# Sixteen-head attention: from two score banks and two banks of turns to three and one, on one core of a Trainium2

## What is computed

```python
# first layer (stage l0a): 16 heads of width 16, masked by a bias on the keys
x = x + _L0_xattn_ref(ctx_2048, _layernorm(x), L0_xattn_b, itok)
# sixth layer (stage l2s): causal self-attention, 16 heads of width 16
scores = jnp.einsum('bhqd,bhkd->bhqk', q, k) * HD ** (-0.5)
scores = jnp.where(causal[None, None], scores, -jnp.inf)
attn = jax.nn.softmax(scores, axis=-1)
ao = jnp.einsum('bhqk,bhkd->bhqd', attn, v)
```

## Time and profile before

| | |
|---|---|
| median of three runs | 3182.69 us (3179.83 to 3188.03) |
| the profiled execution's own time | 3181.22 us |
| its span | 3179.5 us |
| PE busy | 2534.5 us (80%) |
| DVE busy | 2180.8 us (69%) |
| ACT busy | 1264.9 us (40%) |
| POOL busy | 996.3 us (31%) |
| stage l0a, first score to last division | 64.1 to 307.8 us |
| stage l2s, first score to the next stage's first turn | 1941.7 to 2167.1 us |

### The profile page before, as it was taken

The page is one execution under the profiler, slowest core; times in us unless marked ns, Lnnn a source line. Parts: engine busy times, 40 slices in busy tenths (PEclk is TensorE's granted clock), DMA queues, the critical chain, the costliest instruction groups (busy, mean ns, idle before and its releaser), DMA issues. The chain is left out here.

```text
span 3179.5 us, 57281 instructions
## 1 busy us (share of the span) xinstructions
PE 2534.5 (80%) x21348; PEld 1651.8 (52%) x21348; DVE 2180.8 (69%) x5526; ACT 1264.9 (40%) x2260; POOL 996.3 (31%) x1420
## 2 busy tenths in 40 slices
PE   2997285999904497997989876886799999969972
PEld 1443263666603266886556543444466555656662
DVE  6897763666547764766678767997666545867758
ACT  1786353333212313111346654773322222256621
POOL 3442271110066170112656316874000000024330
PEclk9999597999956599998999987998899999989996
DMA  4331266221171026665721022100100000011001
GB/s 104 122 120 58 91 237 203 80 73 63 45 249 31 24 97 233 234 224 185 243 78 48 18 72 82 43 23 6 64 9 12 1 1 1 1 42 52 22 9 58
DMA packets 158167, 266.90 MB, mean 84 GB/s; under 512 B 22635, under 2 KB 106137, under 8 KB 151876
## 3 DMA queue, kind: packets, MB, share of 16 engines
q1 hardware_dynamic: 131204, 186.97, 17.8%
q0 software_dynamic: 17904, 76.23, 7.1%
q10 hardware_dynamic: 8784, 0.04, 0.2%
HBM read 175.25 MB, written 88.34 MB: 83 GB/s over the span
## 5 line engine op out<-in xcount | busy, mean ns | idle before, releaser
L1427 ACT ACTIVATE l2e_hf<-l2e_H 128x512 f32<-128x512 f32 x208 | 124.2, 597 | 376.1 <-PE l2e_H L1383 376.1
L1552 POOL TENSOR_TENSOR all_m_rstd<-all_m_sq,all_mhalf 128x8 f32<-128x8 f32 x18 | 29.6, 1646 | 551.0 <-DVE all_m_sq L1537 550.9
L731 DVE TENSOR_REDUCE l0a_mx<-l0a_S 128x2 f16<-128x512 f32 x256 | 168.3, 688 | 24.0 <-PE l0a_S L565 23.3
L1463 DVE CAST l2e_hh<-l2e_hf 128x512 f16<-128x512 f32 x208 | 88.8, 427 | 125.8 <-ACT l2e_hf L1427 110.7
L727 DVE CUSTOM_DVE_ANT_0 l2s_masked<-l2s_S,l2s_mq 128x128 f32<-128x128 f32 (+1 forms) x512 | 153.2, 349 | 19.9 <-PE l2s_S L565 19.5
L680 ACT ACTIVATE l0a_pf<-l0a_ST 128x512 f32<-128x512 f32 x256 | 146.7, 602 | 45.3 <-PE l0a_ST L579 45.0
L1383 PE MATMUL l2e_H<-l2o_hi,l2e_w 128*128 128x512 f16 x576 | 151.8, 382 | 14.9 <-DVE l2e_w L1439 14.9
L1427 ACT ACTIVATE l0e_hf<-l0e_H 128x512 f32<-128x512 f32 x128 | 76.4, 597 | 207.2 <-PE l0e_H L1383 207.2
L1383 PE MATMUL l2e_H<-l2e_hh,l2e_w 128*128 128x512 f16 x640 | 155.1, 379 | 0.0
L1383 PE MATMUL l1e_H<-l1b_hi,l1e_w 128*128 128x256 f16 (+1 forms) x936 | 144.7, 274 | 7.8 <-DMA l1e_w<-packed,all_second_weight_row 7.8
L1465 DVE TENSOR_TENSOR l2e_hl<-l2e_hf,l2e_hh 128x512 f16<-128x512 f32 x208 | 144.0, 693 | 7.2
(11 more groups left out here) (713 smaller groups left out, 7541.3 us busy)
## 6 DMA issues: line engine op xcount, KB each, us to landing
l0e_wf<-in_L_ffn_w SPq DMA_DIRECT2D x16, 1024.0 KB, 7.2
rows<-l0a_zeros SPq DMA_DIRECT2D x16, 640.0 KB, 5.9
l1u_rb<-rows SPq DMA_DIRECT2D x20, 512.0 KB, 5.2
results<-l1e_y SPq DMA_DIRECT2D x39, 256.0 KB, 3.8
l0a_kv<-in_ctx SPq DMA_DIRECT2D x16, 512.0 KB, 4.1
rows<-l0a_zeros SPq DMA_DIRECT2D x16, 512.0 KB, 4.9
l0d_p_cx<-in_ctx SPq DMA_DIRECT2D x16, 512.0 KB, 6.7
l0u_rb<-rows SPq DMA_DIRECT2D x16, 512.0 KB, 5.7
```

Of the source, the lines that this page charges most:

```text
L731: m = nc.vector.tensor_reduce(mx[h % 2][:, :, i], ps[:, :].rearrange("p (u k) -> p u k", u=TB), AX.X, ALU.max)
L1427: nc.scalar.activation(hf[q % 4][0:fn, :], pair_of(q, lay)[0][0:fn, :], lay.func, scale=1.0 / WS).then_inc(acted, 1)
L1463: nc.vector.tensor_copy(high, v).then_inc(hi_done, 1)
L1552: self.nc.gpsimd.tensor_tensor(out=(self.rstd, self.rstd2)[which][:, g], in0=(self.sq, self.sq2)[which][:, g], in1=self.g.mhalf[:, 0:self. ...
```

## The change

With 16 heads the stage gets a third score bank and gives up the second bank of turns: queries, keys and maxima are all turned in one bank, in that order round, each turn waiting for the copy of the one before. LAG grows from 17 to 19, both halves of `weigh` stand in the same slot (0 and 4, where c = 0 stood in 2 and 6 and c = 1 in 4 and 0), `turn_back` moves from slot 1 to 2, `copy_max` from 4 to 3, `divide` from 3 to 4, `copy_keys` from 1 to 0, and `copy_queries` from slot 0 of the next group to slot 6 of the same group. The stages with 8 heads keep every value.

```diff
-    LAG = heads + 1
+    LAG = 19 if heads == 16 else 9
+    SR = 3 if heads == 16 else 2
     RING, VR, NPF = 6, 5, 3 * G
-    BACK_AT, MAX_AT, TURN_Q_AT, TURN_K_AT = (1, 2, 5, 7) if heads == 16 else (1, 1, 3, 3)
-    COPY_AT, DIV_AT, KEYS_AT, SUM_AT = (4, 3, 1, 5) if heads == 16 else (2, 3, 1, 3)
-    APART = G // 2 if heads == 16 else 0
+    BACK_AT, MAX_AT, TURN_Q_AT, TURN_K_AT = (2, 2, 5, 7) if heads == 16 else (1, 1, 3, 3)
+    COPY_AT, DIV_AT, KEYS_AT, SUM_AT = (3, 4, 0, 5) if heads == 16 else (2, 3, 1, 3)
+    QUERIES_AT, QUERIES_FOR = (6, 2) if heads == 16 else (0, 1)
+    APART = 0
...
-        S_ps = [st.ps(f"S{i}") for i in range(2)]
+        S_ps = [st.ps(f"S{i}") for i in range(SR)]
...
-        MH_ps = [st.ps(f"M{i}", [P, 8, P], F16) for i in range(2)]
+        MH_ps = [st.ps(f"M{i}", [P, 8, P], F16) for i in range(1 if heads == 16 else 2)]
+        if heads == 16:
+            MH_ps = MH_ps * 2
...
-                        if n >= 2:
-                            pe.wait_ge(maxed, n - 1)
-                    m = pe.matmul(S_ps[n % 2][:, s_at[u]:s_at[u] + key_to[u]],
+                        if n >= SR:
+                            pe.wait_ge(maxed, n - SR + 1)
+                    m = pe.matmul(S_ps[n % SR][:, s_at[u]:s_at[u] + key_to[u]],
...
                     if h:
                         pe.wait_ge(q_turned, h)
+                        if heads == 16:
+                            pe.wait_ge(k_turned, h)
                     turn(h, 0)
...
                     if h:
                         pe.wait_ge(k_turned, h)
+                    if heads == 16:
+                        pe.wait_ge(q_turned, h + 1)
                     turn(h, 1)
...
                     pe.wait_ge(q_turned, min(h + 3, NH))
+                    if heads == 16:
+                        pe.wait_ge(k_turned, min(h + 3, NH))
...
-                    ps = S_ps[n % 2]
+                    ps = S_ps[n % SR]
...
-                    if i == 0 and 0 <= j + 1 < NH:
-                        copy_queries(j + 1)
+                    if i == QUERIES_AT and 0 <= j + QUERIES_FOR < NH:
+                        copy_queries(j + QUERIES_FOR)
```

## The result

The changed kernel takes 3188.8 us (median of 20 runs) where the kernel before takes 3183.6 us in the same comparison (20 runs): a ratio of 1.0018, with a 95% interval of 1.0011 to 1.0025. That is 5 us or 0.2% slower. By the bound of 0.3% it counts as no change, but the interval leaves out 1, so the sign is settled. The forecast was 3175 us with a range up to 3185.

A forecast was written before the change was run, and what follows sets the result against it. No engine is full; a loop of waits between TensorE and VectorE sets each group's period. Stage l0a at -11.1 us and l2s at +3.8 us make -7.3 us, so 3175 us against the median of 3182.7, range 3159 to 3185 us.

The forecast's parts named there:

- The old loop: In l0a before: copy of maxima, turn of queries, TensorE to slot 3's score, maximum, division, copy again; 7.15 us per group.
- path B: Loop around one group over ScalarE's copy of the keys and the first exponential: 6.81 us in l0a, 6.52 in l2s.
- Path A: Loop around one group over the paired `weigh` on TensorE and VectorE's maxima: 6.79 us in l0a, 6.36 in l2s.
- So a group of l0a takes 6.80 us.: Period of a group in l0a after the change, 0.35 us less than before; 26 groups give -9.1 us.
- the ring: One bank's cycle: turn of queries, VectorE's copy, turn of keys, ScalarE's copy, turn of maxima, VectorE's copy; handoffs 0.05 us.
- rival 3: Each handoff of the bank costs 0.15 us, not 0.05: +17 us, 3192 us; decides from 0.11 us on; chance 0.06.
- Every second group takes 6.9 us, the mean is 6.71.: In l2s the pair of slot 4 waits for GpSimd's later cuts: 0.16 us more per group, +4.2 us in 26.
- LAG of 19 adds two slots with exponentials alone at each end: At the ends of each stage, slots with exponentials alone cost 0.5 to 0.6 us each: +1.2 us per stage.
- The first four groups: At each stage's start the third score bank frees VectorE: -3.5 and -0.9 us in l0a, -3.3 us in l2s.
- the last two groups: At each stage's end these groups turn nothing and gain: -2.0 us in l0a, -1.5 us in l2s.
- Rival 2: Engines overlap almost fully: groups of l0a at VectorE's 6.15 us and of l2s at 5.88, 3135 us; chance 0.07.
- Rival 4: TensorE's clock falls to 1.2 GHz where it waits more often: 1.9 us more per group, +48 us in one stage; chance 0.02.

## Why the prediction was wrong

**Right.** The old loop ends, and the loop through the one bank of turns sets the period, over two paths that nearly tie (7.00 us over B, 6.93 over A). The pair holds TensorE 156.30 - 155.30 = 1.00 us, VectorE idles 0.63 us (forecast 0.7) ahead of the maximum of slot 1, the copied keys start 0.03 us behind the turn of keys, the start costs 3.2 us in each stage, and l2s loses by GpSimd's stacking in every second group. The run with later copied keys bears out that last step: with the first exponential ahead of the copied keys, l2s goes to 6.40 us in every group.

**Wrong: sizes, all with one sign.** The step that failed is the sum around the loop, above all *"So a group of l0a takes 6.80 us"*. The two stages missed by 11.3 us (+4.0 for -7.3). The other 2.5 us between 3175 and 3188.8 us lie outside them or in the scatter of executions.
- *"So a group of l0a takes 6.80 us."* It takes 7.00, which is 5.3 us in 26 groups. Of the 0.20 us, the handoff from the copy of the queries to the turn of keys makes 0.09: 0.14 us, where I took 0.05 with a bound of 0.10. Turning back and turned maxima took 0.79, the bound, and not 0.73: the overlap of 0.06 us that I called my estimate isn't there. These two lie on path B, which decides; the maxima and the first exponential add the rest, 0.01 to 0.03 us each. Path A by itself is 6.93 us for 6.79: the same handoff, and four maxima at 2.41 for 2.34. The other two handoffs of the ring are 0.03 and 0.06 us. So rival 3 (0.15 us each, all three) has one of its three, and the mean of 0.08 stays below its point of 0.11.
- *"Every second group takes 6.9 us, the mean is 6.71."* It is 6.67 and 6.99, mean 6.83; with the table's +6.2 for +4.2 that is 2.0 us. (The periods alone would give 3.1 us; single groups at both ends of the stretch differ from them, and one group of before took 7.12 us.) The short group has nearly the same handoff, 0.15 us: TensorE starts the turn of keys at 2032.46, the copy ended at 2032.31.
- *"LAG of 19 adds two slots with exponentials alone at each end, ... 1.2 us."* 2.1 and 2.3 us, 2.0 us more in all. I had not costed the pairs there. The end of l0a on ScalarE, after:

```profile
287.88 2.24 ACT L690 ACTIVATE l0a_pf<-l0a_ST 128x512 f32<-128x512 f32 x4 [0.72 <-PE l0a_ST L583]
290.47 0.60 ACT L684 ACTIVATE l0a_oT<-l0a_O 128x512 f32<-128x512 f32 x1 [0.36 <-PE l0a_O L599]
...
296.45 0.60 ACT L684 ACTIVATE l0a_oT<-l0a_O 128x512 f32<-128x512 f32 x1 [0.36 <-PE l0a_O L599]
```

and before:

```profile
295.77 0.60 ACT L674 ACTIVATE l0a_oT<-l0a_O 128x512 f32<-128x512 f32 x1
...
301.49 0.60 ACT L674 ACTIVATE l0a_oT<-l0a_O 128x512 f32<-128x512 f32 x1
```

  Behind each pair ScalarE waits 0.72 us for the next ST. A group at the end takes 296.45 - 290.47 = 5.98 us; before it took 5.72 us. By my estimate from these rows, two slots more at 0.75 us (5.98 / 8) and two groups 0.26 us longer make 2.0 of l0a's 2.1 us; no run separates them.
- *The first four groups* gained 6.2 us in both stages together and not 7.7, and the last two groups 3.0 and not 3.5. Both were worked out with the same short path A; I take that for the cause, without a run for it.

These add up to 11 us, the error of the two stages. The range was too narrow for the same reason: I bounded the handoff (too low, at 0.10 us) and GpSimd's wait and let the other estimates stand, though most were taken at their lower end, and the sum of a loop multiplies such an error by 52 groups.

Two slips in the rivals decided nothing. Rival 2's sum for VectorE in l2s is 5.91 us, not 5.88, and the chance of a gain over 0.3% comes to 0.44, not 0.43. Rival 4 took the price of the low clock from a turn of 1.01 us, but for 60 to 70 us of that trace the granted clock is given as 1.00 too, so that row doesn't show the price.

**What the prediction didn't weigh.** It named three causes for the gain in one sentence ("together they cost less") and never asked what each is worth. The runs did. Three of them and the change make a chain from before to after, in which each line is one run and changes only what it names against the line above it (the usual period of a group in l0a and, on average, in l2s; then the two stages together and the step; all in us):

```
                                          l0a    l2s    stages   step
before                                    7.15   6.55    494.5
copy of maxima first, division later      6.72   6.34    475.6  -18.9
three score banks, one bank of turns,
  copied queries in slot 6                7.01   6.48    490.3  +14.7
pairs, LAG of 19, turning back later      6.93   6.40    485.5   -4.8
copied keys in slot 0 (the change)        7.00   6.83    498.5  +13.0
```

The steps hold in this order and need not in another. With two score banks the pairs cost 0.56 us per group of l0a (7.28 for 6.72), and in the change's own slots 0.28 us (7.00, the run with two banks of turns, whose copied keys are in slot 0 too). So the change is one gain of 19 us and a small one of 5, and two losses, the exchange of banks and the copied keys ahead of the first exponential, that give them back. The prediction foresaw how the copied keys make GpSimd late in l2s, but never asked what slot 1 would give.

The Trainium skill (TensorEngine Tiling, Key Properties) says that a change of tiling mode drains TensorE. The trace still agrees: one such change less is 0.14 us per pair, seen in the 1.00 us above. It is a saving in an engine that isn't the bound. The fall of the clock that rival 4 took up, and that the Trainium skill (TensorE: Matmul & The Clock Gate, A second HAM failure mode: psum-queue depth-cycling) describes for another kernel, didn't come: the granted clock stays 1.00 in both stretches with three score banks.

## What to carry to other kernels

Where two engines are both near 90% busy and wait for each other once per group, find the one instruction that the loop waits for and move that alone first: here a copy of 0.2 us moved ahead of a division of 0.6 us, with the division a slot later, was worth 0.7%, and what was built around it lost the gain again. A bank taken from one use and given to another moved the wait here and didn't remove it; trace the ring of the use that gives before counting what the other gets. Joining two pieces of work saved the engine that does them, but while they lasted the engines fed by it got nothing, so count the banks that are to bridge it. And where a change moves several constants, put each back alone: one of them, a copy of 1.0 us ahead of an exponential that a third engine waits for, cost 13 us of the 19 gained.

## What was not expected

- A handoff isn't one number. From VectorE's copy of 1024 elements (0.68 us by its row) to TensorE's first turn it is 0.14 to 0.15 us; from TensorE's turn to ScalarE's copy 0.03, from an exponential to TensorE 0.06.
- A pair, 128x32 tiles with 16 matmuls, holds TensorE 1.00 us in l0a and 2034.05 - 2033.26 = 0.79 us in l2s (forecast 0.80); where the turned maxima come next it is 159.56 - 158.67 = 0.89 us in l0a (run with pairs and copy first).
- On a third chip one untouched stage took 65 us longer, and the two stages studied here took the same time as on the others, so stage times carried over and whole-kernel times did not. Why that stage is longer there is open.
